# Expert FFN behind a per-batch condition: two shared up products inside the sort, condition ahead of bias, an accumulation kept open at the end, the routed down product split from tile 4

## The reference

```python
h = einsum('bsi,bio->bso', x, W[id]) + b[id][:, None, :]     # condition: one of 16 experts per batch
xf = h.reshape(-1, 256)                                      # 1024 tokens
y = silu(xf @ sw1) * (xf @ sw3) @ sw2                        # shared part, 352 hidden
scores = softmax(xf @ gate_w); weights, indices = top_k(scores, 2)
for e in range(8):                                           # routed part, 176 hidden each
    y = y + cw[:, e:e+1] * (silu(xf @ rw1[e]) * (xf @ rw3[e]) @ rw2[e])
out = x + y.reshape(4, 256, 256)
```

## Time and profile before

| what | value |
|---|---|
| three runs | 113.93, 114.67, 115.14 us (median 114.67) |
| the profiled execution | 114.82 us, its span 113.2 us |
| mean granted TensorE clock | 0.985 of full |
| TensorE busy | 104.1 us (92%) |
| VectorE busy | 68.0 us (60%) |
| ScalarE busy | 52.2 us (46%) |
| GpSimd busy | 47.7 us (42%) |
| chain that ended last | TensorE 60%, ScalarE 8%, VectorE 7%, unknown 7%, DMA 5%, GpSimd 3% |

### The profile page before, as it was taken

One profiled execution on the slowest core, in us unless ns is written; L12 is line 12 of the kernel. 1 busy time (PEld: TensorE's weight loads), 2 busy tenths in 40 slices (PEclk: granted clock), 3 DMA queues, 4 the chain that ended last, 5 costly groups with the idle time before them and its releaser, 6 DMA issues.

```text
span 113.2 us, 2194 instructions
## 1 busy us (share of the span) xinstructions
PE 104.1 (92%) x608; PEld 88.2 (78%) x608; DVE 68.0 (60%) x220; ACT 52.2 (46%) x131; POOL 47.7 (42%) x63
## 2 busy tenths in 40 slices
PE   6997998499999978999999999999999999999870
PEld 4776887466688856677889998999999997888650
DVE  1034864546999079878877775684754533123991
ACT  4044673762660295366655753456556545102200
POOL 5280078872777200005653345335535536703610
PEclk9999999959999999999999999999999999999999
DMA  2897999996988446431232424231021120029935
GB/s 36 247 309 240 349 362 360 372 393 174 228 254 274 185 142 188 125 110 60 93 133 73 143 84 136 88 128 54 5 93 40 52 92 0 0 23 381 376 122 210
DMA packets 16736, 19.07 MB, mean 168 GB/s; under 512 B 2338, under 2 KB 13718, under 8 KB 16726
## 3 DMA queue, kind: packets, MB, share of 16 engines
q1 hardware_dynamic: 13302, 12.62, 36.3%
q0 software_dynamic: 1984, 4.46, 11.2%
q10 hardware_dynamic: 1440, 1.86, 4.9%
HBM read 12.64 MB, written 7.21 MB: 175 GB/s over the span
## 4 chain that ended last, share of the span: by engine, by line
PE 60%; ACT 8%; DVE 7%; another core or an unknown queue 7%; issue 6%; DMA 5%; POOL 3%; POOLq 1%; DVEq 0%; ACTq 0%
PE bank L858 42%; PE bank L870 6%; DVE x_area L815 5%; PE bank L1027 4%; PE bank L992 4%; ACT w_all L494 4%; DMA y_area<-_out_by_choice_and_token 3%; ACT cond_area L462 2%; DMA _out_by_choice_and_token<-y_area,dest 2%; ACT hT_area L443 1%; PE bank L885 1%; PE bank L888 1%; POOL _out_by_choice_and_token L412 1%; POOLq L289 1%
## 5 line engine op out<-in xcount | busy, mean ns | idle before, releaser
L412 POOL DMA_INDIRECT _out_by_choice_and_token<-y_area,dest x23 | 23.6, 1025 | 38.0 <-DVE y_area L771 26.3
L858 PE MATMUL bank<-w_all,hsT_hi 128*128 x72 | 21.6, 342 | 0.0
L396 POOL DMA_INDIRECT rows_by_expert<-h_area,slot x16 | 15.7, 978 | 12.8 <-DVE slot L634 8.7
L858 PE MATMUL bank<-hT_area,sh_area 128*128 128x512 f32 (+1 forms) x72 | 18.6, 418 | 0.0
L858 PEld LDWEIGHTS bank<-hT_area,sh_area 128*128 128x128 f32 (+1 forms) x72 | 13.4, 190 | 4.1 <-DVE sh_area L552 0.3
L858 PEld LDWEIGHTS bank<-w_all,hsT_hi 128*128 128x128 f32 x72 | 13.0, 188 | 0.0
L765 DVE TENSOR_TENSOR y_area<-y_area,bank 128x176 f32<-128x176 f32 x23 | 7.7, 336 | 7.3 <-issue 4.2
L509 ACT ACTIVATE y_area<-bank 128x176 f32<-128x176 f32 x23 | 7.3, 317 | 10.2 <-PE bank L858 8.3
L552 DVE TENSOR_TENSOR hsT_lo<-bank,hsT_hi 128x256 fp32r<-128x256 f32 x18 | 7.6, 423 | 6.7 <-ACT hsT_hi L505 5.5
L858 PE MATMUL bank<-w_all,hsT_lo 128*128 x36 | 11.5, 320 | 0.0
L858 PE MATMUL bank<-sh_raw,gated 128*128 128x256 f32 (+1 forms) x48 | 10.8, 380 | 0.6 <-DVE gated L567 0.6
(11 more groups left out here) (130 smaller groups left out, 200.3 us busy)
## 6 DMA issues: line engine op xcount, KB each, us to landing
h_area<-rows_by_expert SPq DMA_DIRECT2D x23, 128.0 KB, 2.0
raw<-in_L_ffn_rw_dram SPq DMA_DIRECT2D x16, 176.0 KB
raw<-in_L_ffn_rw_dram SPq DMA_DIRECT2D x2, 704.0 KB
rows_by_expert<-x_area SPq DMA_DIRECT2D x8, 128.0 KB
y_area<-_out_by_choice_and_token SPq DMA_DIRECT2D x4, 256.0 KB, 4.6
...
```

The lines of the kernel that those rows point to most:

```text
L396: nc.gpsimd.indirect_dma_start(out=rows_dram, out_offset=bass.IndirectOffsetOnAxis(ap=slot[:, i, t:t + 1], axis=0), in_=h_sb[:, t, :], in_ ...
L412: nc.gpsimd.indirect_dma_start(out=y_dram, out_offset=bass.IndirectOffsetOnAxis(ap=dest[:, j:j + 1], axis=0), in_=y_sb[j % NBY], in_offset ...
L858: last = nc.tensor.matmul(dst, w, v, start=start and n == 0, stop=stop and n == len(operands) - 1)
```

## The change

It has five parts that do not depend on each other in what they compute.

1. GpSimd writes `expert_no` ahead of its other early work, and TensorE makes the first half of the first condition product ahead of the bias products.
2. TensorE's first shared up product stands between the last condition product and `h_by_token(2)`, and the second one ahead of the last ranks. VectorE makes `sh_lo` of block 0, and GpSimd that of block 1.
3. `FIRST_DOWN` is 4 instead of 11. ScalarE rounds four experts of `w2_hi` ahead of the tile loop, behind a wait for the last shared up product (its memory is that of `hT`), and two each in steps 0 and 1. GpSimd makes all of `w2_lo` ahead of its scatters.
4. The shared down products of batch 2 and of the second half of batch 3 leave their accumulation open in PSUM, and the diagonal products are added on top. ScalarE's copies and GpSimd's adds of the tail are gone. VectorE adds the shared part of the first half of batch 3.
5. The shared down products stand in another order, and the six idle products ahead of the rows write to another bank.

```diff
-    FIRST_DOWN = 11
+    FIRST_DOWN = 4
     HI13, LO13, ROW = 0, KD * F2, 2 * KD * F2
...
-        y_acc = [[bank[1][:, 0:D], bank[5][:, D:2 * D]]] + [[bank[n][:, 0:D], bank[n][:, D:2 * D]] for n in (4, 7, 6)]
-        acc_ps = [None] + [bank[n][:, :] for n in (4, 7, 6)]
-        weighed_ps = [[bank[0][:, 0:D], bank[2][:, 0:D]], [bank[1][:, 0:D], bank[3][:, 0:D]]]
+        y_acc = [[bank[1][:, 0:D], bank[5][:, D:2 * D]], [bank[4][:, 0:D], bank[4][:, D:2 * D]],
+                 [bank[0][:, 0:D], bank[2][:, 0:D]], [bank[1][:, 0:D], bank[3][:, 0:D]]]
...
             pool.dma_start(ids_bc[:, :], ids.to_broadcast([NE, B])).then_inc(ids_in, 16)
+            nc.gpsimd.iota(expert_no[:, :], pattern=[[0, 1]], base=0, channel_multiplier=1).then_inc(expert_no_ready, 1)
             pool.wait_ge(ident_ready, 1)
             nc.gpsimd.affine_select(out=ident[:, :], in_=ident[:, :], compare_op=ALU.not_equal, fill=1.0,
                                     base=0, pattern=[[-1, P]], channel_multiplier=1).then_inc(ident_ready, 1)
             condition_in(pool, nc.gpsimd, 2)
-            nc.gpsimd.iota(expert_no[:, :], pattern=[[0, 1]], base=0, channel_multiplier=1).then_inc(expert_no_ready, 1)
             pool.wait_ge(ident_ready, 2)
...
             dispatch(0)
-            pool.wait_ge(sh_hi_ready, 1)
-            nc.gpsimd.tensor_tensor(sh_lo[:, :, shared_cols(0)], sh_raw[:, :, shared_cols(0)],
-                                    sh_hi[:, :, shared_cols(0)].bitcast(F32), ALU.subtract).then_inc(sh_lo_pool, 1)
+            pool.wait_ge(sh_hi_ready, 2)
+            nc.gpsimd.tensor_tensor(sh_lo[:, :, shared_cols(1)], sh_raw[:, :, shared_cols(1)],
+                                    sh_hi[:, :, shared_cols(1)].bitcast(F32), ALU.subtract).then_inc(sh_lo_pool, 1)
             for b in range(1, B):
...
+            for e in range(E):
+                pool.wait_ge(w2_hi_ready, e + 1)
+                nc.gpsimd.tensor_tensor(w2_lo[:, e, :], raw2_rows[:, e, :], w2_hi[:, e, :].bitcast(F32), ALU.subtract) \
+                    .then_inc(w2_lo_ready, 1)
             pool.wait_ge(dest_ready, 1)
             for j in range(NTILE):
                 scatter(j)
-            for b in range(BH, B):
-                pool.wait_ge(acc_sb_ready, b - BH + 1)
-                x_row = x_sb[:, b].rearrange("p j d -> p (j d)")
-                nc.gpsimd.tensor_tensor(x_row, acc_sb[b - BH][:, :], x_row, ALU.add).then_inc(late_base_ready, 1)
...
-            def w2_hi_of(e):
-                if e == 0:
-                    act.wait_ge(raw2_in, 16 * 2)
-                nc.scalar.copy(w2_hi[:, e, :], raw2_rows[:, e, :]).then_inc(w2_hi_ready, 1)
             def late_y_of(j):
                 act.wait_ge(y_ps_ready, j + 1)
                 act.wait_ge(scattered[j % NBY], 16 * (j // NBY))
                 nc.scalar.copy(y_sb[j % NBY], y_ps[j % 2]).then_inc(late_y_ready, 1)
+            def w2_hi_of(e):
+                if e == 0:
+                    act.wait_ge(b_ready, len(groups))
+                    act.wait_ge(raw2_in, 16 * 2)
+                nc.scalar.copy(w2_hi[:, e, :], raw2_rows[:, e, :]).then_inc(w2_hi_ready, 1)
+            for e in range(E // 2):
+                w2_hi_of(e)
             hsT_of(0)
...
                     late_y_of(s - 2)
-                if 1 <= s <= E:
-                    w2_hi_of(s - 1)
+                if 0 <= s < 2:
+                    w2_hi_of(E // 2 + 2 * s)
+                    w2_hi_of(E // 2 + 2 * s + 1)
             for i in range(NBY):
                 act.wait_ge(scattered[i], 16 * len(range(i, NTILE, NBY)))
             read_rows(act, 1)
-            for b in range(BH, B):
-                act.wait_ge(acc_ready, JS * (b + 1))
-                nc.scalar.copy(acc_sb[b - BH][:, :], acc_ps[b]).then_inc(acc_sb_ready, 1)
...
             hT_lo_of(2, 1)
+            sh_lo_of(0)
             hT_lo_of(3, 0)
...
                 lo_part(gT_lo[j % 2][:, :], gT_ps[j % 2], gT_hi[j % 2][:, :]).then_inc(gT_lo_ready, 1)
-            def w2_lo_of(e):
-                dve.wait_ge(w2_hi_ready, e + 1)
-                lo_part(w2_lo[:, e, :], raw2_rows[:, e, :], w2_hi[:, e, :]).then_inc(w2_lo_ready, 1)
...
                     w13_lo_of(s + 4)
-                if 2 <= s < E + 2:
-                    w2_lo_of(s - 2)
                 if E + 4 <= s < E + 4 + NT // 2 and s - E - 4 + NT // 2 != JS * (B - 1):
                     diagonals_of(s - E - 4 + NT // 2)
-            base_of(0, 1)
-            dve.wait_ge(acc_ready, JS * BH)
+            base_of(0, 1, 2)
+            dve.wait_ge(acc_ready, 2 * JS)
             x_row = x_sb[:, 1].rearrange("p j d -> p (j d)")
-            nc.vector.tensor_tensor(x_row, acc_ps[1], x_row, ALU.add).then_inc(base_ready, 1)
+            nc.vector.tensor_tensor(x_row, bank[4][:, :], x_row, ALU.add).then_inc(base_ready, 1)
+            base_of(B - 1, 0, 2 * JS + 1)
...
                     dve.wait_ge(weighed_ready, min(JS * (b - BH) + j + 1, JS + 1))
-                    nc.vector.tensor_tensor(x_sb[:, b, j, :], weighed_ps[b - BH][j], x_sb[:, b, j, :], ALU.add) \
+                    nc.vector.tensor_tensor(x_sb[:, b, j, :], y_acc[b][j], x_sb[:, b, j, :], ALU.add) \
                         .then_inc(out_ready, 1)
         @block.tensor
         def _(pe):
-            def keep_warm(times):
+            def keep_warm(times, unused=2):
                 for _ in range(times):
-                    nc.tensor.matmul(bank[2][:, 0:2 * P], nc.const_aps.tensor(1.0, [P, P], BF16),
+                    nc.tensor.matmul(bank[unused][:, 0:2 * P], nc.const_aps.tensor(1.0, [P, P], BF16),
                                      nc.const_aps.tensor(1.0, [P, 2 * P], BF16), start=True, stop=True)
...
                 toks = slice(b * S + j * P, b * S + (j + 1) * P)
-                last = add_products(y_acc[b][j],
-                                    [(gated[0:shared_rows(c), c, toks], sh2_raw[0:shared_rows(c), c, :])
-                                     for c in range(NSH)], True, True)
-                last.then_inc(acc_ready, 1)
+                add_products(y_acc[b][j], [(gated[0:shared_rows(c), c, toks], sh2_raw[0:shared_rows(c), c, :])
+                                           for c in range(NSH)], True, b < BH or (b, j) == (B - 1, 0)).then_inc(acc_ready, 1)
...
             turn_x(1)
+            condition(0, 0)
             pe.wait_ge(one_hot_ready, 1)
             pe.wait_ge(bias_in, 16)
             for m in range(KD):
                 last = nc.tensor.matmul(bias_ps[:, m * B:(m + 1) * B], bias_rows[:, m * P:(m + 1) * P], one_hot[:, :],
                                         start=True, stop=True)
             last.then_inc(bias_ps_ready, 1)
-            condition(0, 0)
             condition(0, 1)
...
             condition(3, 1)
+            shared_up(0, 0)
             h_by_token(2)
             h_by_token(3)
-            shared_up(0, 0)
+            shared_up(0, 1)
             ranks(2)
-            shared_up(0, 1)
             for g in range(1, len(groups)):
...
             shared_down(0, 1)
-            for b in range(1, B):
-                for j in range(JS):
-                    shared_down(b, j)
+            for j in range(JS):
+                shared_down(1, j)
             pe.wait_ge(late_y_ready, NTILE - FIRST_DOWN)
+            shared_down(B - 1, 0)
+            for j in range(JS):
+                shared_down(B - 2, j)
+            shared_down(B - 1, 1)
             pe.wait_ge(diagonal_ready, TOPK * (JS * (B - BH) - 1))
-            keep_warm(WARM_BEFORE_ROWS)
+            keep_warm(WARM_BEFORE_ROWS, 6)
             for b in range(BH, B):
                 pe.wait_ge(y_in[b], 16 * TOPK)
                 for j in range(1 if b == B - 1 else 0, JS):
-                    add_products(weighed_ps[b - BH][j], [(diagonal[b - BH][j][i][:, :], y_tok[:, b, i, j * D:(j + 1) * D])
-                                                         for i in range(TOPK)], True, True).then_inc(weighed_ready, 1)
+                    add_products(y_acc[b][j], [(diagonal[b - BH][j][i][:, :], y_tok[:, b, i, j * D:(j + 1) * D])
+                                               for i in range(TOPK)], False, True).then_inc(weighed_ready, 1)
```

17 lines of the change are left out of this document (6 added, 11 removed).

## The result

| kernel, session | time, us | ratio to before, 95% interval |
|---|---|---|
| before, first session | 114.45 median of 4 | |
| changed, first session | 116.16 median of 4 (116.09 to 118.28) | 1.0132 [1.0068, 1.0196] |
| changed again, second session | 113.80 median of 12; before 113.43 of 35 | 0.9998 [0.9925, 1.007] |

What follows compares the result with a forecast made beforehand. It took TensorE to bound the tile loop, with late ScalarE ahead of it and VectorE's weighing behind it. Terms 0 + 0.1 - 1.0 + 0.2 - 0.6 = -1.3 us gave 113.5, as a median 113.4; range 110.5 to 115.2.

Steps and rivals of the forecast that it cites:

- `w2_lo` to GpSimd: Tile loop: GpSimd makes eight `w2_lo` ahead of its scatters; price 0 if done by 58.7, +0.2 us for slowed VectorE.
- Down split: Tile loop: tiles 4 to 10 at 2.12 us a step instead of 2.26, -1.0 us in all.
- Six shared up passes into the pause: Sort: TensorE's pause of 1.92 us shrinks, the clock stays up, ranks, slots and dispatch come about 1.1 us earlier.
- The dispatch at 26.4: Sort: GpSimd dispatches by the slots from about 26.4, where before it began at 27.53.
- ScalarE at the loop's start: Start of tile loop: ScalarE resumes at 37.9, four `w2_hi` precede `hsT`, which starts at 44.1 to 44.2; +0.1 us.
- the late silu: Shared up: the fourth silu, at 38.97 before after 5.56 us idle on ScalarE, expected at 37.9 with the earlier dispatch.
- rival B: Loop start slips: clock falls again or queues run dry no earlier; `hsT` at 45.25, +1.25, total 114.5; chance 0.20.
- Front: Ahead of the token products: condition earlier, bias later, first `hT_hi` at 8.2 instead of 8.0; 0 to +0.2, taken as 0.
- Tail: After the tile loop: VectorE loses two waits of 1.0 us, then rows and diagonal products bind it; -0.6 us.
- the last rows landing after 107.3: Tail, a listed sign of a wrong prediction: rows read back after 107.3, where the sum counted on 106.81.
- A: Shared up: the late silu moves with ScalarE's program (-3.2, 111.5) or goes (-5.0, 109.7); chance 0.30.
- C: Tile loop: GpSimd's products pass 58.7 and hold up TensorE; at 2.5 us each +2.7, 117.4; chance 0.12.

Runs made afterwards that it cites:

- D alone: The kernel before with only the down split of part 3 added: 1.0038 of before in a session without stills, 1.0192 in one with stills.
- the tail alone: The kernel before with only parts 4 and 5 of the change added: 0.9993 of before, in a session without stills.

## Why the prediction was wrong, point by point

- **The step that failed: "`w2_lo` to GpSimd ... Price 0 as long as GpSimd is done by 58.7."** It was done at 56.3, TensorE's tile 4 did not wait for it, and the price was not 0. For the loop I had -1.0 and +0.2; the trace has +1.0. The seven shorter steps did give their 1.0. Against that stand 0.50 for `w2_hi` in the second step (I had nothing), 0.35 for the slow `w13_lo` (I had 0.2), and 1.1 for the stall in steps 7 and 8 (0.32 and 0.81 above 2.12; I had nothing). As a whole, part 3 measured +1.9% (2.2 us) in a session with stills. I asked whether the consumer would wait and whether the queue would catch up. I did not ask what catching up does: four scatters back to back, beside which ScalarE stands still for 1.1 to 2.6 us. It does so in all five traces of sessions with stills that have such a burst, and in the others it has no such still near 60 us. In a session without stills D alone had five scatters back to back and ScalarE did not stop. That both come together is shown; by what means one holds up the other is not, and neither is what makes up the rest of the 1.9%, since D's one trace there has a span only 0.9 us longer than that of before (114.1 against 113.2, in different sessions).
- *Its sizes.* 1.75 us a product against 1.33 to 1.52: the end was 1.4 to 2.9 later than forecast, and the first scatter 5.1 later, not 2 to 4. VectorE's `w13_lo` grew to 1.45 and the last ended at 55.2; TensorE lost 0.35 in that step, inside my bounds of 0 to 0.7. Where VectorE made `w2_lo` itself, `w13_lo` took 0.88 again. The rule of the Trainium skill ("SBUF — State Buffer", shared port pair), that the two block each other for a whole instruction, fits both sizes, and the tail's four weighs in 1.67 with GpSimd silent.
- *Down split.* Right in itself: every undisturbed step with it took 2.11 to 2.12. But "two a step in steps 0 and 1, ... less than a step" was wrong: the second step took 2.89 to 2.99 instead of 2.49 in every trace with two `w2_hi` in it, except where the clock was low. That is 0.4 to 0.5 of the 1.0.
- *Six shared up passes into the pause.* The clock was right (1.00). The dispatch at 26.4 was wrong (28.16): VectorE waited instead. In sessions without stills there is no pause to fill, and the same passes put off the slots by 1.1 us, on a path that had that much room.
- *ScalarE at the loop's start.* `hsT` 43.91 against 44.1 to 44.2, right by luck. "Its program up to the late silu is the same" was wrong: the fifth silu was late, not the fourth, so less was left behind it. Its resumption at 37.9 was wrong too (39.51), but not the reading that it goes with the dispatch: the dispatch came 0.6 later instead of 1.1 earlier, and so did ScalarE. With the block and no moved product `hsT` came at 45.08 in one trace, near rival B's 45.25, and at 43.65 to 43.96 in three, in which the late silu resumed at 37.4 to 37.7.
- *Front.* Forecast 0 to +0.2 at the first `hT_hi` (8.2) and taken as 0. It starts at 8.44 to 8.54 in the six traces that have this part, and at 7.98 to 8.35 in the other fourteen. TensorE's pause did not take it up: the sixteen dispatches begin at 14.77 instead of 14.34, so 0.4 of the dispatch's later 0.6 was there before the sort. The part was not timed alone.
- *Tail.* The two waits of VectorE went, as said. The last rows bound it, as said, but they came at 109.5, not 106.81: "the last rows landing after 107.3" was on the list of what would prove me wrong. Part of it is the sixth packet of code, which I had not seen. TensorE's program is longer by fourteen passes and their weight loads, and this was in no term of the sum. Reads with the packet had their first weigh 3.56 to 4.42 us after the first issue, without it 3.21 to 3.62 (seven and thirteen traces): some 0.5 us, where I had forecast -0.6. And without the packet the gain is small: from the last `y` to the end it is 16.36 with the tail alone, and 16.55 and 17.08 in the two traces of before.
- *Rivals.* A did not happen: the still ended with the dispatch, at another instruction. In sessions without stills no kernel traced has a late silu, with moved products or without. B's start came once in four, as told above. C had the right engine, place and sign, at a chance of 0.12, but not the mechanism: its products were to pass 58.7, and they did not.

One version came out under before, narrowly and in one session with stills: the change without part 3, at 0.994.
